# First attention of a two-layer kernel: a score block as one stacked product in place of three

## What is computed

```
q   = layernorm(x) @ w_q                  # 16 heads of 16
k,v = split(ctx @ w_kv)                   # one key and value of 16 for all heads, 77 rows
score = q_h @ k.T / 4                     # per head h
prob  = softmax(score)
out   = concat_h(prob @ v) @ w_concat     # added to x
```

## Time and profile before

| | |
|---|---|
| median of 3 runs | 862.39 us |
| the profiled execution: its own time | 862.12 us |
| its span, first to last instruction | 860.4 us |
| TensorE busy, of the span | 764.5 us (89%) |
| VectorE busy | 597.3 us (69%) |
| ScalarE busy | 496.8 us (58%) |
| GpSimd busy | 292.0 us (34%) |
| DMA traffic | 139.02 MB |

### The profile page before, as it was taken

How to read it: one execution, slowest core, us unless ns; L and a number is a source line. 1 busy time by engine, 2 the same in 40 slices (tenths; PEclk the granted TensorE clock), 3 DMA queues, 4 the chain that set the end, 5 groups by cost and what they waited for, 6 DMA issues and landing times.

```text
span 860.4 us, 14192 instructions
## 1 busy us (share of the span) xinstructions
PE 764.5 (89%) x5047; PEld 664.1 (77%) x5047; DVE 597.3 (69%) x1071; ACT 496.8 (58%) x858; POOL 292.0 (34%) x294
## 2 busy tenths in 40 slices
PE   3899999996799999999999999997878748897984
PEld 3566776674699999999999999996756547897974
DVE  4766555266577878786868868775687686767746
ACT  1366465422466767776767767675273564766740
POOL 7266455510213131322213122221341016777440
PEclk9999999999699999999999999999997868999997
DMA  5000010011666767785857766752600076888847
GB/s 168 1 1 0 1 50 32 18 50 50 215 227 202 246 225 234 253 282 180 290 174 265 236 244 220 261 198 87 202 2 0 1 245 215 263 259 249 240 132 245
DMA packets 56551, 139.02 MB, mean 162 GB/s; under 512 B 6946, under 2 KB 25763, under 8 KB 56483
## 3 DMA queue, kind: packets, MB, share of 16 engines
q1 hardware_dynamic: 48994, 117.67, 41.6%
q0 software_dynamic: 7488, 20.46, 7.4%
HBM read 117.39 MB, written 20.71 MB: 161 GB/s over the span
## 4 chain that ended last, share of the span: by engine, by line
PE 52%; DVE 18%; issue 9%; POOL 8%; ACT 6%; DMA 6%; SPq 1%; POOLq 0%; DVEq 0%; ACTq 0%
PE ps L326 47%; DVE w_lo L1152 6%; POOL p_lo L658 5%; DMA wr<-in_w1gu 4%; ACT w_hi L754 3%; PE ps L2160 1%; DVE h_lo L1152 1%; POOL a_lo L637 1%; PE ps L2116 1%; DMA wr<-y_d 1%; DVE x_all L1780 1%; PE ps L2254 1%; DVE t_lo_a L1152 1%; DMA xnb<-xm_d,gat 0%; DVE st_a L1597 0%
## 5 line engine op out<-in xcount | busy, mean ns | idle before, releaser
L1152 DVE TENSOR_TENSOR w_lo<-wr,w_hi 128x1024 fp32r<-128x1024 f32 (+2 forms) x193 | 221.6, 1161 | 57.3 <-ACT w_hi L754 56.6
L754 ACT ACTIVATE w_hi<-wr 128x1024 fp32r<-128x1024 f32 (+2 forms) x193 | 192.0, 999 | 24.1 <-DMA wr<-in_w1gu 18.9
L326 PE MATMUL ps<-xe_hi,w_hi 128*128 128x256 f32 x600 | 173.5, 289 | 2.7 <-DVE xe_lo L1152 1.4
L326 PE MATMUL ps<-xe_lo,w_hi 128*128 128x256 f32 x600 | 170.9, 285 | 0.0
L326 PE MATMUL ps<-xe_hi,w_lo 128*128 128x256 f32 x600 | 170.8, 285 | 0.0
L679 POOL DMA_INDIRECT y_d<-ye,sca x39 | 43.4, 1113 | 276.8 <-ACT ye L913 272.2
L326 PE MATMUL ps<-w_hi,h_hi 128*128 128x256 f32 x422 | 125.9, 298 | 11.6 <-DVE h_lo L1152 10.6
L326 PEld LDWEIGHTS ps<-xe_hi,w_hi 128*128 128x128 f32 x600 | 116.3, 194 | 5.6 <-DVE xe_lo L1152 4.0
L326 PE MATMUL ps<-w_lo,h_hi 128*128 128x256 f32 x422 | 120.5, 285 | 0.0
L326 PE MATMUL ps<-w_hi,h_lo 128*128 128x256 f32 x422 | 120.3, 285 | 0.0
L326 PEld LDWEIGHTS ps<-xe_lo,w_hi 128*128 128x128 f32 x600 | 116.3, 194 | 0.0
(11 more groups left out here) (334 smaller groups left out, 1553.7 us busy)
## 6 DMA issues: line engine op xcount, KB each, us to landing
wr<-in_w SPq DMA_DIRECT2D x144, 512.0 KB, 4.5
wr<-in_w1gu SPq DMA_DIRECT2D x24, 512.0 KB, 5.0
wr<-in_w1d SPq DMA_DIRECT2D x24, 256.0 KB, 3.2
xn_d<-xnb SPq DMA_DIRECT2D x8, 512.0 KB, 3.5
wr<-y_d SPq DMA_DIRECT2D x8, 512.0 KB, 7.5
x_all<-in_x SPq DMA_DIRECT2D x4, 512.0 KB, 5.6
xm_d<-xnb SPq DMA_DIRECT2D x4, 512.0 KB, 4.1
xnb<-y_d SPq DMA_DIRECT2D x4, 512.0 KB, 5.7
```

What stands on the lines that cost most here:

```text
L326: return nc.tensor.matmul(out, w, x, start=start, stop=stop, skip_group_check=True)
L754: return s.activation(o, i, ACT.Copy)
L1152: return v.tensor_tensor(o, a, b, ALU.subtract)
```

## The change

The three products of a score block become one. A block of at most 128 columns touches only two heads, so 32 of a unit's 96 query rows; three terms of 32 rows and the six rows of maxima make 102, as many as before. For this the blocks are cut anew within halves of three heads (`TRIO` = 231 columns): 128, 103, 128 and 103 columns, of heads 0-1, 1-2, 3-4 and 4-5 (77 columns for the last of a unit of four heads); their number stays 44. In `k_st` and `q_st` rows 0 to 31 hold the term hi·hi, 32 to 63 `lo` keys by `hi` queries, 64 to 95 `hi` keys by `lo` queries, 96 to 101 the -1 and the maxima.

`q_st` has its own 512 columns for each block. Since engines can't move data across partitions like this, SyncE does: per unit it stores `q_hi` and `q_lo` to memory (`q_d`, 192 KB each for six heads), and when both have landed and unit u−2's score blocks are done, loads six pieces of 32 rows by 2 by 512 (128 KB each) into `q_st`; the ninth transfer copies the maxima, six rows broadcast to the four blocks (48 KB), after `place_max`. A unit's first score block waits for all seven.

The setup changes with it: `k_lo` goes, `k_st` comes (made from a new masked product `kraw3`), the five zero fills on GpSimd go and four small fills come, and `q_hi`, `q_lo` gain waits for the transfers that read them three units before. The `p` tiles move to another place in memory.

```diff
+            def stack(u):
+                p, k, h = u % 2, HEADS_OF[u] * DH, HEADS_OF[u]
+                if u >= 2:
+                    sp.wait_ge(qs_in[p], stacked(u - 2))
+                for i, (q, ready) in enumerate(((q_hi, q_hs), (q_lo, q_ls))):
+                    sp.wait_ge(ready, u + 1)
+                    sp.dma_start(q_d[p, i, 0:k, :], q[0:k, u % HG, :].bitcast(f32)).then_inc(qd_st, 16)
+                if u >= 2:
+                    sp.wait_ge(s_mm, FIRST[u - 1])
+                sp.wait_ge(qd_st, 32 * (u + 1))
+                for part, i in enumerate((0, 0, 1)):
+                    for b in range(2):
+                        ... q_st[32 rows of part, p, blocks of parity b] <- q_d[p, i, ...] .then_inc(qs_in[p], 16)
+                sp.wait_ge(mt_ok, u + 1)
+                sp.dma_start(q_st[QS:QS + h, p, :, :] <- q_hi[UK:UK + h, u % HG, :] broadcast to NW).then_inc(qs_in[p], 16)
+            stack(0)
+            stack(1)
+            for g in range(NG + 2):
+                if g < NG:
+                    stack(HG * g + 2)
+                if g >= 2:
+                    ... the two stores of xn_d of group g - 2
+                if g + 1 < NG:
+                    stack(HG * g + 3)
+                    stack(HG * g + 4)
@@ GpSimd, start
+            g.memset(even3[...]) x4 .then_inc(const_ok, 1)
-            link(g.memset(q_hi[UK:UM, :, :].bitcast(f32), 0.0))      # and q_lo, k_lo, and
-            link(g.memset(q_hi[P // 2:UK, HG - 1, :].bitcast(f32), 0.0))  # the same of q_lo
@@ ScalarE, start
             queries_hi(0)
-            act.wait_ge(v_raw, 1)
+            act.wait_ge(k_raw, 2)
+            for b in range(BATCH):
+                ins = copy(k_st[0:QS, b, :, :], kraw3[:, b:b + 1, :].to_broadcast([QS, TU, TRIO]))
+            ins.then_inc(kv_hi, 1)
+            act.wait_ge(k_raw, 3)
             copy(v_hi[:, :, :, :], vraw[:, :, :, :]).then_inc(kv_hi, 1)
@@ VectorE, start
-                v.tensor_copy(k_hi[UK:UM, b, :], nege[:, :])
+                v.tensor_copy(k_st[QS:QM, b, :, :].rearrange("p w n -> p (w n)"), nege[:, :])
+            link(v.tensor_tensor(even ...)) x2, link(v.tensor_scalar(pair3 ...))
+                ins = v.tensor_tensor(kraw3[:, b, :] ..., pair3 ..., ALU.mult)      # x2
@@ VectorE, after rows_lo(0), ahead of block_values()
-            dve.wait_ge(kv_hi, 1)
-            sub(k_lo[0:UK, :, :], kraw[:, :, :], k_hi[0:UK, :, :])
+            dve.wait_ge(kv_hi, 2)
+            lo = slice(2 * DH, 4 * DH)
+            for b in range(BATCH):
+                sub(k_st[lo, b, :, :], kraw3[lo, b:b + 1, :].to_broadcast([2 * DH, TU, TRIO]), k_st[lo, b, :, :])
@@ TensorE, scores(b)
                 if j == 0:
-                    pe.wait_ge(q_ls, u + 1)
-                    pe.wait_ge(mt_ok, u + 1)
-                out, cols = ps[0:w, b % 2, :], slice(P * j, P * j + w)
-                mm(out, k_hi[:, bt, cols], q_hi[:, u % HG, :], True, False)
-                mm(out, k_lo[:, bt, cols], q_hi[:, u % HG, :], False, False)
-                mm(out, k_hi[:, bt, cols], q_lo[:, u % HG, :], False, True).then_inc(s_mm, 1)
+                    pe.wait_ge(qs_in[u % 2], stacked(u))
+                mm(ps[0:w, b % 2, :], k_st[:, bt, j // 2, P * (j % 2):P * (j % 2) + w], q_st[:, u % 2, j, :], True, True
+                   ).then_inc(s_mm, 1)
```

More of the change, by code:

```diff
@@ L20 @@
 NW = -(-UW // P)
+TRIO = 3 * NKEY
+TU = HU // 3
+FROM = [TRIO * (j // 2) + P * (j % 2) for j in range(NW)]
+QS = 3 * 2 * DH
+QM = QS + HU
 NU = NG * HG
@@ L90, in build_program @@
         y1_d = nc.dram_tensor("y1_d", [YROWS, D], f32).ap()
+        q_d = nc.dram_tensor("q_d", [2, 2, UK, GW], f32).ap()
         out_d = A["out"]
@@ L196, in build_program @@
         wc_hi, wc_lo = sb("wc_hi", [UK, HG, D], f32r, a0), sb("wc_lo", [UK, HG, D], f32r, a0)
-        q_hi, q_lo = sb("q_hi", [UM, HG, GW], f32r, a0), sb("q_lo", [UM, HG, GW], f32r, a0)
-        p32 = sb("p32", [P, 3, GW], f32, a0)
-        p_hi, p_lo = sb("p_hi", [P, 4, GW], f32r, a0), sb("p_lo", [P, 4, GW], f32r, a0)
+        q_hi, q_lo = sb("q_hi", [UM, HG, GW], f32r, a0), sb("q_lo", [UK, HG, GW], f32r, a0)
+        q_st = sb("q_st", [QM, 2, NW, GW], f32r, a0)
         top_t = sb("top_t", [P, 2, GT, HU], f32, a0)
@@ L205, in build_program @@
         a32 = sb("a32", [UK, 2, GW], f32, a0)
-        k_hi, k_lo = sb("k_hi", [UM, BATCH, UW], f32r, a0), sb("k_lo", [UM, BATCH, UW], f32r, a0)
+        k_hi = sb("k_hi", [UK, BATCH, UW], f32r, a0)
+        k_st = sb("k_st", [QM, BATCH, TU, TRIO], f32r, a0)
         v_hi, v_lo = sb("v_hi", [P, BATCH, NW, UM], f32r, a0), sb("v_lo", [P, BATCH, NW, UM], f32r, a0)
@@ L213, in build_program @@
         kraw = sb("kraw", [UK, BATCH, UW], f32, early)
+        kraw3 = sb("kraw3", [QS, BATCH, TRIO], f32, early)
+        nege, bd = sb("nege", [HU, UW], f32, early), sb("bd", [UK, UW], f32, early)
+        even, even3, pair3 = sb("even", [UK, 1], f32, early), sb("even3", [UK, TRIO], f32, early), sb("pair3", [UK, TRIO], f32, early)
         vraw = sb("vraw", [P, BATCH, NW, UM], f32, early)
         early.close()
+        p32 = sb("p32", [P, 3, GW], f32, a0)
+        p_hi, p_lo = sb("p_hi", [P, 4, GW], f32r, a0), sb("p_lo", [P, 4, GW], f32r, a0)
         a_lo = sb("a_lo", [UK, 2, HG, GW], f32r, a0)
@@ L279, in build_program @@
         pool_ch, dve_ch = sem("pool_ch"), sem("dve_ch")
[L280 to L281 removed]
+        wk_ok, ctx_ok, k_mm, k_raw, kv_hi, kv_lo = (sem(n) for n in (
+            "wk_ok", "ctx_ok", "k_mm", "k_raw", "kv_hi", "kv_lo"))
         ws0_hi, ws0_lo = sem("ws0_hi"), sem("ws0_lo")
[L283 to L284 removed]
+        qs_in, qd_st = [sem(f"qs_in{p}") for p in range(2)], sem("qd_st")
+        kp_mm, kp_sb, g_mm, vg_hi, vg_lo = (sem(n) for n in (
+            "kp_mm", "kp_sb", "g_mm", "vg_hi", "vg_lo"))
         q_mm, q_hs, q_ls, mx_mm, mx_ok, mt_mm, mt_ok, s_mm, p_ex, p_ls, pv_mm = (sem(n) for n in (
@@ L429, in build_program, with stacked @@
                 turns_w += [(t + 1, 2), (t + 1, 3)] + ([(t + 1, 4), (t + 1, 5)] if SPAN[t + 1] == 2 else [])
+        def stacked(u):
+            return 16 * 7 * (u // 2 + 1)
         def parted(t, b):
@@ L776, in queries_hi @@
                 act.wait_ge(q_mm, u + 1)
+                if u >= HG:
+                    act.wait_ge(qs_in[(u - HG) % 2], stacked(u - HG))
                 copy(q_hi[0:k, u % HG, :], ps[0:k, bank_of("q", u + 1), :]).then_inc(q_hs, 1)
@@ L1187, in _ @@
             v.memset(zpad[:, :], 0.0)
-            v.memset(vraw[:, :, NW - 1, 0:UK], 0.0)
+            for j in (1, NW - 1):
+                v.memset(vraw[:, :, j, 0:UK], 0.0)
             dve.wait_ge(x_first, 16)
             statistics(na, tile_of(0))
-            dve.wait_ge(const_ok, 2)
+            dve.wait_ge(const_ok, 3)
             for b in range(BATCH):
-                v.tensor_copy(k_hi[UK:UM, b, :], nege[:, :])
+                v.tensor_copy(k_st[QS:QM, b, :, :].rearrange("p w n -> p (w n)"), nege[:, :])
+            link(v.tensor_tensor(even[:, :], bd[:, 0:1], bd[:, 2 * NKEY:2 * NKEY + 1], ALU.add))
+            link(v.tensor_tensor(even[:, :], even[:, :], bd[:, 4 * NKEY:4 * NKEY + 1], ALU.add))
+            link(v.tensor_scalar(pair3[:, :], even3[:, :], even[:, :], None, ALU.is_equal))
             dve.wait_ge(k_mm, 1)
@@ L1199, in _ @@
             ins.then_inc(k_raw, 1)
+            for b in range(BATCH):
+                ins = v.tensor_tensor(kraw3[:, b, :].rearrange("p (h k) -> p h k", k=NKEY),
+                                      ps[0:QS, 0:1, b * NKEY:(b + 1) * NKEY].to_broadcast([QS, 3, NKEY]),
+                                      pair3[:, :].rearrange("p (h k) -> p h k", k=NKEY), ALU.mult)
+            ins.then_inc(k_raw, 1)
             normalise(na, 0, tile_of(0))
@@ L1227, in queries_lo @@
                 dve.wait_ge(q_hs, u + 1)
+                if u >= HG:
+                    dve.wait_ge(qs_in[(u - HG) % 2], stacked(u - HG))
                 sub(q_lo[0:k, u % HG, :], ps[0:k, bank_of("q", u + 1), :], q_hi[0:k, u % HG, :]).then_inc(q_ls, 1)
@@ L1242, in place_max @@
                 dve.wait_ge(mt_mm, u + 1)
-                v.tensor_copy(q_hi[UK:UK + HEADS_OF[u], u % HG, :], ps[0:HEADS_OF[u], bank_of("t", u + 1), :]).then_inc(mt_ok, 1)
+                if u >= HG:
+                    dve.wait_ge(qs_in[(u - HG) % 2], stacked(u - HG))
+                h = HEADS_OF[u]
+                v.tensor_copy(q_hi[UK:UK + h, u % HG, :], ps[0:h, bank_of("t", u + 1), :]).then_inc(mt_ok, 1)
             def invert_sums(u):
```

52 lines of the change are left out of this document (27 added, 25 removed).

## The result

The changed kernel is slower: 876.44 us, median of 4 runs (872.62 to 876.84), against 863.19 us for the kernel before (4 runs, 861.95 to 864.6), a ratio of 1.0148 with a 95% interval of 1.0127 to 1.017. Forecast were 857.2 us and a range of 850 to 867 us. The profiled execution took 876.53 us, its span is 874.8 us. In the ratios of this document, executions more than 1.5% above the fastest one of their kernel are left out; that concerns two of the seven of e10 alone, whose median is of all seven.

The account below looks back on a forecast made before the run. TensorE was taken to set the pace of groups 1 to 3, a ScalarE and GpSimd chain close behind. -13.8 + 4.4 + 1.8 + 2.4 = -5.2 us gave 857.2 us against the median; range 850 to 867 us.

Parts of the forecast that it names:

- Step 3: TensorE after the idle start: half-level clock lasts into blocks 2 to 5, costing 1.8 us, bounds 0 to 5.
- Step 1: Score blocks: two products fewer each free 19.3 us of TensorE, 13.8 us kept; bounds 9.7 to 19.3.
- rival B: Attention groups: ScalarE and GpSimd chain sets the pace, half the saving kept, 861.3 us, no change; chance 0.2.
- The loss at the ten spreads: Spreads in the attention: each follows a chain that shortens less than TensorE's blocks, losing 0.46 us each.
- Step 2: Lead-in: `x_a` 1.0 us earlier, but VectorE waits for ScalarE's `k_st` copies; 4.4 us late, bounds 3.0 to 6.0.
- Only the 4.4 us pass on: Unit 0's first block: comes at 39.9 us, not 34.18, but meets the same wait for unit 1's maxima.
- step 4: The nine transfers per unit: eight stay hidden, the ninth stalls units 3 and 10, 2.4 us in all; upper 7.5.
- d: Time from placed maxima to a unit's started first block, taken as 2.4 us, bounds 2.0 to 3.6.
- rival A: Each unit's first block: transfers come too late; gain gone at 3.6 us from placed maxima, 868 us at 4.5; chance 0.22.
- the first three: Signs: unit 0's `q_lo` at about 31 us, first score block near 40, 0.43 us cadence past 40 us.
- the waits and the groups: Signs: DMA waits at units 3 and 10 alone, 1 to 2 us; groups 1 and 2 shorter by 3 to 4 each.
- Behind the attention nothing changes: Rest of the span after the attention: no change in time.

Follow-up runs that it names:

- e10: Changed kernel with e2's copy order and the maxima of units 3g+1 and 3g+3 one step earlier, no unused products: 862.48 us, ratio 0.9984 to the kernel before.
- e3: Changed kernel plus unused 512-column products where TensorE waits, ahead of units 0, 3, 4, 7, 10 and at three steps per group: 864.8 us, ratio 1.0025 to the kernel before.
- e2: Changed kernel with ScalarE's two copies to `k_st` moved ahead of unit 0's `queries_hi`: 868.42 us, ratio 1.0062 to the kernel before.
- e7: Changed kernel with e2's copy order and e3's unused products together: 857.47 us, ratio 0.9952 to the kernel before.
- e5: Kernel before with the two `lo` products left out of every score block, no transfers or new waits: 866.31 us, ratio 1.0034 to the kernel before.
- e9: e5 plus e3's 3, 4 and 6 unused products per group: 857.96 us, ratio 0.9956 to the kernel before.
- e8: Changed kernel with e2's copy order, maxima of units 3g+1 and 3g+3 one step earlier, and fewer unused products than e3: 856.35 us, ratio 0.9926 to the kernel before.
- e4: Changed kernel with each stacked product issued three times, so TensorE's work is the old one: 879.34 us, ratio 1.0187 to the kernel before.
- e1: Changed kernel with transfers of units 0 and 1 only; later units reread the old `q_st`, so scores are wrong: 876.12 us, ratio 1.0151 to the kernel before.

## Why the prediction was wrong, step by step

**Step 3, the clock, failed worst: taken at 1.8 us, bounds 0 to 5, measured at about 10** (9.9 us between the profiled executions of the changed kernel and e3, 11.6 us between their medians). I looked at the half level only as a leftover of the idle start. That part came as forecast: the clock was at the half level up to 45.1 us. But five more stretches followed all through the attention, and from 40 us on they make 32.4 us together. Four pairs that differ in the unused products alone agree in sign: changed kernel to e3 -1.2%, e2 to e7 -1.1%, e5 to e9 -0.8%, e10 to e8 -0.6%.

Two things bring the half level on. One is blocks that got shorter between chains that did not: e5 has no transfer and no new wait, and had 28.8 us of it, of which only 1.4 us are the start's leftover. The other is the waits for the transfers: e4 has the old number of products and had 20.2 us, and from e2 to e10, with shorter waits, 14.5 us went. From group 3's first block on TensorE was busy 32.70 of 34.70 us before, at a clock of 1.00; in e5 30.85 of 35.10 us at 0.82, with no wait above 2.1 us; and with unused products (e9) 31.91 of 34.00 us, again at 1.00. So TensorE's small number of holes was itself what held the clock, and the change took it away. How small it must be is not shown: e5's group 2 was busy 33.15 of 36.10 us and kept the full clock. No rival had this mechanism.

The Trainium skill (TensorE: Matmul & The Clock Gate, A second HAM failure mode: psum-queue depth-cycling) tells of a kernel whose TensorE idles for short moments between groups of products, so that its clock goes to and fro between the levels. The traces agree: besides the start's there are four stretches in e5, whose waits were no longer than 2.1 us. The same page's rule against long idle gaps (HAM oscillation — how this bites in real kernels) would not have warned of e5.

**Step 1, mis-sized: kept 13.8 of 19.3 us, measured 4 to 9.** e5's group 2 at full clock keeps 2.35 of 5.1 us, 46%; over 42 blocks that would be 8.9 us, near rival B's half. With the unused products that hold the clock it is less: 3.8 us by e9's ratio, and 4.1 us in groups 1 to 3 of e3 against the kernel before. The loss at the ten spreads, put at 10 x 0.46 = 4.6 us, was about right: the waits for `wide` grew from 2.9 us to 7.8 in e5, by 4.9 us. What the step left out is the rest, some 5 us and more. TensorE's waits that are put down to VectorE's maxima (`top_t`) grew from 1.9 to 5.0 us in e5, and those for the placed maxima from 0.7 to 1.9; how much of this is the half level's and how much the shorter blocks' no run took apart. By the rule on weight loads that the prediction weighed (Perfetto Trace Analysis of the Trainium skill) rival B should have been nearer, and at full clock it was.

**Step 2, right on VectorE, wrong on what passes on.** `q_lo` of unit 0 started at 30.34 us, forecast 31.2; `x_a` at 11.99, forecast 12.95; VectorE's wait for the copies was where it was put. So VectorE was 3.5 us later than before, not 4.4, and unit 1's maxima, done at 39.82 us, were too. But the first block came at 40.85 us, forecast 39.9, because its transfer took longer than step 4 had it (below). "Only the 4.4 us pass on" failed there: the wait for unit 1's maxima no longer covered the late first block. TensorE's program runs in order, so it turned these maxima only at 41.84 us, 2.0 us after they were done and 5.5 us later than in the earlier trace rows. e2 undid the order of the copies, brought the first block 5.5 us forward and won 0.85%, 7.4 us; its profiled execution lay 5.4 us above the median of its runs and does not show where the other 1.9 us are.

**Step 4, half right.** The eight earlier transfers fitted, and no wait is put down to them. The ninth took 4.26 us at unit 0, 4.11 at unit 3, about 3.45 at units 4, 7 and 10 and 4.18 at unit 11, from placed maxima to started block, not 2.4; no run shows how much of it comes from its few source rows. So d stood around rival A's turning point of 3.6 us. Besides unit 0's wait of 3.7 us there were 7.0 us over five units where 2.4 were forecast over two. But A is not the cause of the whole: with these d its own sum loses 6.4 us more than the forecast, which gives 863.6 us and not 876, and e1 without the waits is as slow as the changed kernel. The share that the waits do have is the 0.8% between e2 and e10.

**The sum again**, by e3, whose clock is full: +6.3 us at the start, +1.0 in group 0, -4.1 in groups 1 to 3, +1.3 behind make +4.5 us. The clock adds 9.9 us: 14.4. e4 gives the same from the other side: some 16 us of costs in place of 8.6, and 3 us kept in place of 13.8. Of the prediction's own signs the first three came, `q_lo`, the first block and the pace past 40 us; the waits and the groups did not, for group 1 was 2.8 us longer and group 2 only 0.7 us shorter, where 3 to 4 us each had been forecast. "Behind the attention nothing changes" was off by 1.4 us in the profiled executions, but this part lay between 694.2 and 702.4 us in the runs of the table, and where its own stretches of half level fall, and why, is left open. Whether they also make the spread of e5's runs (861.15 to 872.14 us) is not shown either.

## What to carry to other kernels

When TensorE is dense and other engines' chains run close behind it, price a removed product by the slack of these chains, and look at the granted clock before counting any gain: work taken out between fixed waits can cost as much as it saved (e5). Where the clock falls in the trace after, test it with unused products in the holes; if the time falls, either keep the fewest that hold the clock or shorten the waits themselves. An operand that arrives by a transfer needs its last input one step earlier than one that an engine writes in place, and a copy that another engine waits for goes ahead of instructions that wait themselves.

## What the hardware showed that I had not expected

- TensorE at the half level with waits of no more than 2.1 us around it (e5, 28.8 us of it), and at the full level again with at most 13 unused products a group (e9). And 20.2 us of it with the old number of products, where TensorE waited for transfers (e4).
- The transfer of six rows broadcast four times (48 KB) occupied its queue 0.79 us at unit 3, against 0.42 us for a load, and it was 3.4 to 4.3 us from placed maxima to the product that reads them, at units 0, 3 and 11 above even the 3.5 us landing of 512 KB.
- Issuing each stacked product three times cost only 0.4% (e4 against the changed kernel), for 88 more products.
